# Second feed-forward layer as one block, with fetched and sent expert rows

## The chip, the cores and the metric

The kernel runs on one core of one Trainium2 chip. The metric is the device time of one execution in microseconds (us). Five engines run their own instruction streams and meet only through semaphores: PE (TensorE, matrix products), DVE (VectorE), ACT (ScalarE), POOL (GpSimd, which here also issues every indirect DMA) and SP (SyncE, which only issues DMAs).

## What is computed

Two layers, each a cross-attention and a mixture-of-experts feed-forward, all residual, on 2048 tokens of 256 numbers. The change is in the last part, the feed-forward of the second layer (15 experts, 3 per token, and one shared expert that every token passes):

```
logits = xt @ gate_w.T
scores = jax.nn.softmax(logits, axis=-1)
topk_w, topk_idx = jax.lax.top_k(scores, TOPK)
topk_w = topk_w / (jnp.sum(topk_w, axis=-1, keepdims=True) + 1e-20)
comb = jnp.zeros((T, E), xt.dtype).at[jnp.arange(T)[:, None], topk_idx].add(topk_w)
h = jnp.einsum('td,efd->etf', xt, fc1_w) + fc1_b[:, None, :]
xh, g = (h[..., :F], h[..., F:])
a = jax.nn.gelu(g, approximate=False) * xh * geglu_mult[:, None, :]
yexp = jnp.einsum('etf,edf->etd', a, fc2_w) + fc2_b[:, None, :]
y = jnp.einsum('etd,te->td', yexp, comb)
hs = xt @ s_fc1_w.T + s_fc1_b
xs, gs = (hs[..., :FS], hs[..., FS:])
as_ = jax.nn.gelu(gs, approximate=False) * xs * s_geglu_mult
ys = as_ @ s_fc2_w.T + s_fc2_b
return (y + ys).reshape(s, b, d)
```

with T = 2048, E = 15, TOPK = 3, F = 256, FS = 512.

## The kernel before

Layer 0 (`layer0`, `experts0`) and the attention of layer 1 (`layer1`) come first; they keep the normalised tokens in `XF` (16 tiles of 128 tokens), their transpose in `XFT`, and the residual stream in `X`. Then three blocks follow, each closed by a barrier over all engines.

`route1` ranks the token-expert pairs by expert and gives each a row (slot) in a table of 62 tiles of 128 rows, where every tile belongs to one expert. DVE does the softmax, the top three and the running counts (`pick`, `softmax_top`), PE adds the counts over the partitions (`rk`), DVE turns them into slots. POOL then scatters the rows of `XF` into the table `xs1` in DRAM with 48 indirect DMAs (L1888), 128 rows each. Beside it runs the shared expert: the tokens are cut in four elements `c` of 512 tokens; for each, PE makes four column pieces (`shared_in`, L1905), ACT the gelu, DVE the gated product `AT` (L1986), then PE the second product for four tiles of 128 tokens (`shared_out`, L1917 to L1921, with two short products that add the shared bias and the weighted expert biases), and DVE adds it to `X` (L2034). SP loads the small vectors and shared weights, then the expert weights `W1` and `W2`, all at the start of this block; ACT multiplies `W2` by the gate's factors (L1963).

`experts1` takes the 62 tiles in order. For each, SP loads the rows `XS` (L2079), PE turns them (`turn`, TP, L2101), multiplies by the expert's first weights (`first`, H, L2110), DVE adds the bias (HB, L2191), ACT does the gelu, DVE the product A (L2197), PE turns it (`turn_back`, TA, L2119) and multiplies by the second weights (`second`, Y, L2128), DVE copies Y into `YS` (`keep`, L2204), and POOL stores it into the table `ys1` (L2088). The engines are staggered: in step `s` PE does `turn(s+1)`, `first(s)`, `turn_back(s-1)`, `second(s-2)`, and DVE does `bias(s)`, `gated(s)`, `keep(s-2)`. XS and YS have four buffers each (`DEEP = 4`). The expert of a tile is read into a register by every engine that indexes a weight or a bias with it (`value_load`).

`combine` gathers the three rows of each token from `ys1` with 48 indirect DMAs on POOL (L1234) and DVE adds each times its weight to `X` (L1245); SP stores the result.

The lines that set the order in one step of `experts1`, on SP and on POOL:

```
sp.wait_ge(xt_ready, j - DEEP + 1)
sp.dma_start(XS[:, c, :], xs_tiles[j]).then_inc(xs_loaded[c], 16)

pool.wait_ge(y_done, j + 1)
pool.dma_start(ys_tiles[j], YS[:, c, :]).then_inc(y_stored[c], 16)
```

## Time and profile before

| | us |
|---|---|
| median of 3 runs (1479.38 to 1481.75) | 1479.79 |
| the profiled execution, its own time | 1479.18 |
| span of its records | 1477.4 |
| from the start of routing to the first expert tile | 158.36 |
| the 62 expert tiles | 205.65 |
| from the last expert tile to the end | 73.39 |

A busy time is the sum of an engine's instructions; a wait is an engine's idle time before an instruction, with what ended it. The share of an engine in the whole span says little here, since the layer's three blocks each have a limit of their own: they are read one by one.

### The profile page before, as it was taken

Reading aid. Unit: us, or ns where it says so; the run is one execution under the profiler, and the core shown is the slowest. Engines: PE = TensorE matmul, PEld = TensorE weight load, DVE = VectorE, ACT = ScalarE, POOL = GpSimd, SP = SyncE. Lnnn points to the kernel's source line nnn. Section 1 sums busy time; section 2 is a strip of 40 time slices with the busy share of each in tenths; the row PEclk is TensorE's granted clock in tenths of the full one; section 3 lists DMA queues with packets and bytes.
Section 4 is the critical chain, followed back from the end, with each engine's and each line's share of the span. In section 5 each row is a group of like instructions: output and inputs, shape, how many; then the busy total and the mean of one; then the engine's idle time right before and its main releaser. Section 6 shows DMA issues by size and latency. Waiting matters only on the chain. (4 is left out here: it accounts for less than half of the span.)

```text
span 1477.4 us, 20683 instructions
## 1 busy us (share of the span) xinstructions
PE 1175.2 (80%) x6778; PEld 768.4 (52%) x6779; DVE 732.5 (50%) x1364; ACT 521.5 (35%) x1084; POOL 399.5 (27%) x482
## 2 busy tenths in 40 slices
PE   4798993699999999944698989997539989999900
PEld 2323442699999999932243534443325455555500
DVE  5576622355665556453776676751421124444423
ACT  1285550344543345300265454644130112222200
POOL 3153456223332223023121120000066001111156
PEclk9698655799999999975699999979759999999955
DMA  3460101322333222034232231200853112222134
GB/s 97 171 264 23 51 27 43 109 93 72 112 122 112 82 70 81 19 111 128 72 112 91 73 102 52 66 1 1 261 184 142 54 47 82 82 82 78 64 103 132
DMA packets 86460, 135.49 MB, mean 92 GB/s; under 512 B 18504, under 2 KB 55468, under 8 KB 86258
## 3 DMA queue, kind: packets, MB, share of 16 engines
q1 hardware_dynamic: 72050, 92.58, 19.6%
q0 software_dynamic: 14336, 41.94, 8.2%
q8 instruction: 45, 0.74, 0.2%
q14 instruction: 29, 0.24, 0.1%
HBM read 86.98 MB, written 47.71 MB: 91 GB/s over the span
## 5 line engine op out<-in xcount | busy, mean ns | idle before, releaser
L1744 DVE TENSOR_REDUCE M<-S 128x2 f32<-128x1024 f32 x128 | 153.9, 1221 | 39.2 <-PE S L1389 35.1
L1651 ACT ACTIVATE PT<-S 128x512 f32<-128x512 f32 x256 | 138.8, 594 | 83.1 <-PE S L1413 81.3
L2110 PE MATMUL H<-W,XST 128*128 x248 | 122.1, 616 | 5.2 <-issue 5.1
L222 POOL TENSOR_TENSOR w12l<-stage,w12h 128x1024 fp32r<-128x1024 f32 x28 | 67.9, 2427 | 202.2 <-ACT w12h L216 202.1
L1197 DVE TENSOR_TENSOR HTm0l<-HFm,HTm0h 128x320 fp32r<-128x320 f32 x128 | 121.7, 951 | 1.0
L1203 DVE TENSOR_TENSOR HFm<-Um,SGm 128x320 f32<-128x320 f32 x128 | 62.4, 487 | 80.9 <-ACT SGm L1166 80.6
L1166 ACT ACTIVATE SGm<-Gm 128x320 f32<-128x320 f32 x128 | 55.9, 437 | 119.0 <-PE Um L1124 118.1
L2088 POOL DMA_DIRECT2D ys<-YS x62 | 33.5, 541 | 233.2 <-DVE YS L2204 233.2
L1137 PE MATMUL Ym<-w3h,HTm0h 128*128 128x256 f32 x320 | 93.3, 292 | 0.0
L909 DVE TENSOR_REDUCE M<-S 128x2 f32<-128x1024 f32 x64 | 77.1, 1222 | 30.4 <-PE S L426 29.9
L1389 PE MATMUL S<-KS,QS 48*128 48x512 f32 x256 | 70.3, 547 | 25.7 <-DVE M L1744 9.5
L1137 PE MATMUL Ym<-w3h,HTm0l 128*128 128x256 f32 x320 | 90.4, 283 | 0.0
L1137 PE MATMUL Ym<-w3l,HTm0h 128*128 128x256 f32 x320 | 90.4, 283 | 0.0
L1426 PE MATMUL PV<-PT,VA 128*32 128x256 f32 x1024 | 85.7, 410 | 5.4 <-issue 3.5
L1124 PE MATMUL Gm<-XSTm0h,w12h 128*128 128x320 f32 x256 | 82.2, 321 | 7.9 <-DVE HFm L1203 6.7
L2191 DVE TENSOR_TENSOR HB<-H,B 128x512 f32<-128x512 f32 x62 | 42.9, 692 | 84.5 <-PE H L2110 84.5
L783 ACT ACTIVATE PT<-S 128x512 f32<-128x512 f32 x128 | 69.3, 594 | 32.3 <-PE S L448 31.9
L1124 PE MATMUL Gm<-XSTm0l,w12h 128*128 128x320 f32 x256 | 79.7, 311 | 0.0
L1124 PE MATMUL Gm<-XSTm0h,w12l 128*128 128x320 f32 x256 | 79.7, 311 | 0.0
L1124 PE MATMUL Um<-XSTm0h,w12h 128*128 128x320 f32 x256 | 79.6, 311 | 0.0
L1124 PE MATMUL Um<-XSTm0h,w12l 128*128 128x320 f32 x256 | 79.6, 311 | 0.0
L1124 PE MATMUL Um<-XSTm0l,w12h 128*128 128x320 f32 x256 | 79.6, 311 | 0.0
(273 smaller groups left out, 2485.0 us busy)
## 6 DMA issues: line engine op xcount, KB each, us to landing
stage<-in_W12T SPq DMA_DIRECT2D x32, 512.0 KB, 6.2
xs<-zeros POOLq DMA_DIRECT2D x25, 512.0 KB, 5.9
stage<-in_W3T SPq DMA_DIRECT2D x16, 512.0 KB, 3.8
XS<-xs SPq DMA_DIRECT2D x62, 128.0 KB, 2.0
ys<-YS POOLq DMA_DIRECT2D x62, 128.0 KB, 2.0
W<-in_fc1T SPq DMA_DIRECT2D x2, 3840.0 KB, 21.8
KS<-scrk SPq DMA_DIRECT2D x96, 64.0 KB, 2.3
QS<-scrq SPq DMA_DIRECT2D x96, 64.0 KB, 2.2
```

What stands on the lines that cost most here:

```text
L222: pool.tensor_tensor(ew.part(1, s, c), ew.stage[:, c % STAGES, :], ew.part(0, s, c).bitcast(F32), ALU.subtract).then_inc(ew.low_done, 1)
L783: act.activation(PT[:, at % SLICES, h + j, :], S2[:, j, :], ACT.Exp, scale=(D / H0) ** -0.5).then_inc(exp_done, 1)
L909: dve.tensor_reduce(M[:, n % 3, at:at + TPB + 1:TPB], out[:, :, :], AX.X, ALU.max).then_inc(S1.done(("max", c)), 1)
L1124: m = pe.matmul(bank[:, c % 2, 0:HALF], ew.w12[a][s][:, k, f:f + P], XST[b][:, k, half * HALF:(half + 1) * HALF], start=(k == 0 and (a, b) ...
L1137: m = pe.matmul(Y[:, (s * NTE + i) % 2, 0:D], HT[a][:, j, i * P:(i + 1) * P], ew.w3[b][s][:, j, :], start=(j == 0 and (a, b) == PASSES[0]) ...
L1197: dve.tensor_tensor(HT[1][:, j, at], HF[:, c % HFS, :], HT[0][:, j, at].bitcast(F32), ALU.subtract).then_inc(h_done, 1)
L1203: dve.tensor_tensor(HF[:, c % HFS, :], U[:, c % 2, 0:HALF], SG[:, c % 2, :], ALU.mult).then_inc(hf_done, 1)
L1389: m = pe.matmul(out[:, j, :], QS[at, n % SLOTS1, hp, q * P:(q + 1) * P], KS[at, n % SLOTS1, hp, :], start=True, stop=True)
L1426: m = pe.matmul(PV[VW * h:VW * (h + 1), at], VA[:, b % 2, kt, GH * g + h, :], PT[:, (4 * n + kt) % SLICES, h, at], start=(kt == 0 and part ...
L1651: act.activation(PT[:, at % SLICES, 2 * hp + j, :], S2[:, j, :], ACT.Exp, scale=HP ** -0.5).then_inc(exp_done, 1)
L1744: dve.tensor_reduce(M[:, n % 3, at:at + 2 * TPB + 1:2 * TPB], out[:, :, :], AX.X, ALU.max).then_inc(S1.done(("max", c)), 1)
L2110: m = pe.matmul(H[:, c % 2, :], XST[:, c % 2, k, :], W1[:, k, bass.ds(e, 1), :], start=(k == 0), stop=(k == KD - 1))
```

## The change

`route1`, `experts1` and `combine` become one block, `ffn1`, without a barrier inside.

- The rows of `XF` are stored in token order in DRAM (`xf1`), by SP during the attention (`xf_stored`), and the shared expert's weights and small vectors are loaded there too (`load_shared`); POOL folds the factor into `s2` there. The zero fill of `xs1` in layer 0 (16 DMAs) goes.
- No row is scattered ahead. Instead the routing makes, for each of the 62 tiles, the list of its 128 tokens: DVE marks each pair's partition and tile (`hot`, six chunks), POOL multiplies by the pair's number, PE adds up with one-hot products (`place`, eight products a chunk), and DVE decodes the table into `moves.source` and `moves.target`.
- In the expert loop POOL fetches a tile's rows with an indirect DMA (`fetch`) and sends its results with another (`send`) straight to the row of the pair in `yk1`. The loop's weights and biases are indexed as before; the second bias is added in `keep`, which reads the expert's number too.
- Of the shared expert, elements 0 to 2 are done before the experts (`FRONT = 3`) and element 3 behind them. The two short bias products are gone; the shared bias is added to `X` by POOL (`shared_bias`).
- At the end SP loads the three rows of each token from `yk1` with plain DMAs (16 of 384 KB), and DVE adds them between the pieces of element 3.

```diff
             fills = [(dram, r, min(ZROWS, rows_ - r), done) for dram, rows_, done in (
-                (env.xs0, E0 * CAP0, filled0), (env.xs1, TILES1 * P, filled1)) for r in range(0, rows_, ZROWS)]
+                (env.xs0, E0 * CAP0, filled0),) for r in range(0, rows_, ZROWS)]
 
...
+                for b in range(BATCH):
+                    if t == ends(b) + 6:
+                        sp.wait_ge(xn_done[1], b + 1)
+                        sp.dma_start(env.xf.rearrange("(b t p) d -> b p t d", p=P, t=TPB)[b],
+                                     XF[:, b % 2 * TPB:(b % 2 + 1) * TPB, :]).then_inc(env.xf_stored, 16)
+                if t == 40:
+                    load_shared()
+            sp.wait_ge(env.xf_stored, 16 * BATCH)
...
+FRONT = 3
+HALVES = 2
+CHUNKS = K1 * HALVES
+TC = NT // HALVES
...
-            for t in range(NT):
-                for k in range(K1):
-                    pool.indirect_dma_start(
-                        out=env.xs1[:, :], out_offset=bass.IndirectOffsetOnAxis(ap=env.slot1[:, k, t:t + 1], axis=0),
-                        in_=XF[:, t, :], in_offset=None).then_inc(env.scattered, 16)
...
-                    pe.matmul(pw[:, t % 2, 0:D], env.ones[0:1, :], s2b[:, :], start=False, stop=False)
-
-                    pe.matmul(pw[:, t % 2, 0:D], combT[:, t * P:(t + 1) * P], f2b[:, :],
-                              start=False, stop=True).then_inc(ys_ready, 1)
...
-                if not (isinstance(r, int) and j < DEEP):
-                    sp.wait_ge(xt_ready, j - DEEP + 1)
-                sp.dma_start(XS[:, c, :], xs_tiles[j]).then_inc(xs_loaded[c], 16)
...
+            for k in range(KF):
+                sp.dma_start(W2[:, k, :, :], ins["fc2T"].rearrange("e (k p) d -> k p e d", p=P)[k]).then_inc(w2_loaded, 16)
+            for k in range(KD):
+                sp.dma_start(W1[:, k, :, :], ins["fc1T"].rearrange("e (k p) f -> k p e f", p=P)[k]).then_inc(w1_loaded, 16)
+            sp.wait_ge(decoded, 1)
+            sp.dma_start(B1[:, :, :], ins["fc1_b"].partition_broadcast(P)).then_inc(b1_loaded, 16)
+            sp.wait_ge(expert_done, 1)
+            sp.dma_start(B2[:, :, :], ins["fc2_b"].partition_broadcast(P)).then_inc(b2_loaded, 16)
+
+            sp.wait_ge(h_ready, TILES1)
+            for c in range(DEEP):
+                sp.wait_ge(y_sent[c], LAST_YS[c])
+            for t in range(NT):
+                sp.dma_start(YK[:, t, :, :], env.yk.rearrange("(k t p) d -> t p k d", k=K1, p=P)[t]).then_inc(yk_loaded[t], 16)
+            for i, t in enumerate(finished):
+                sp.wait_ge(fin, i + 1)
+                sp.dma_start(out.rearrange("(t p) d -> t p d", p=P)[t], env.X[:, t, :]).then_inc(sent, 16)
+            sp.wait_ge(sent, 16 * NT)
...
-                pool.dma_start(ys_tiles[j], YS[:, c, :]).then_inc(y_stored[c], 16)
...
+            for i in range(CHUNKS):
+                k, h = divmod(i, HALVES)
+                pool.wait_ge(hot_done, i + 1)
+                wait(pool, hot_free, i - 1)
+                pool.tensor_tensor(HV[:, i % 2, :, :], HI[:, i % 2, :, :],
+                                   env.moves.val[:, k, h * TC:(h + 1) * TC].unsqueeze(2).to_broadcast([P, TC, TILES1]),
+                                   ALU.mult).then_inc(hv_done, 1)
+
+            def fetch(j):
+                if j >= DEEP:
+                    pool.wait_ge(xt_ready, j - DEEP + 1)
+                pool.indirect_dma_start(
+                    out=XS[:, j % DEEP, :], out_offset=None, in_=env.xf[:, :],
+                    in_offset=bass.IndirectOffsetOnAxis(ap=env.moves.source[:, j:j + 1], axis=0),
+                ).then_inc(fetched[j % DEEP], 16)
+
+            def send(j):
                 pool.wait_ge(y_done, j + 1)
-                pool.dma_start(ys_tiles[j], YS[:, c, :]).then_inc(y_stored[c], 16)
-
-            steps(pool, step)
-            for c in range(DEEP):
-                pool.wait_ge(y_stored[c], 16 * ((TILES1 - c + DEEP - 1) // DEEP))
+                pool.indirect_dma_start(
+                    out=env.yk[:, :], out_offset=bass.IndirectOffsetOnAxis(ap=env.moves.target[:, j:j + 1], axis=0),
+                    in_=YS[:, j % DEEP, :], in_offset=None, bounds_check=K1 * TOK - 1, oob_is_err=False,
+                ).then_inc(y_sent[j % DEEP], 16)
+
+            pool.wait_ge(env.xf_stored, 16 * BATCH)
+            pool.wait_ge(decoded, 1)
+            for j in range(DEEP):
+                fetch(j)
+            for c in range(2, BATCH):
+                shared_bias(c)
+            for j in range(TILES1):
+                if j + DEEP < TILES1:
+                    fetch(j + DEEP)
+                send(j)
...
+            def place(i):
+                pe.wait_ge(hv_done, i + 1)
+                for t in range(TC):
+                    m = pe.matmul(table, LO[:, i % 2, t, :], HV[:, i % 2, t, :], start=(i == 0 and t == 0),
+                                  stop=(i == CHUNKS - 1 and t == TC - 1))
+                m.then_inc(hot_free, 1)
+
+            shared_in(0, 0)
+            shared_in(0, 1)
+            pe.wait_ge(run_done, 1)
+            pe.matmul(rk[:, 0:NT, :], env.before[:, :], w.all[:, :, :], start=True, stop=False)
+            pe.matmul(rk[:, 0:NT, :], env.ones[:, :], w.run[:, 0:NT, :], start=False, stop=True)
+            pe.matmul(rk[:, NT, :], env.ones[:, :], w.run[:, NT, :], start=True, stop=True).then_inc(rk_ready, 1)
+            shared_in(0, 2)
+            shared_in(0, 3)
+            place(0)
+            place(1)
+            for q in range(TPB):
+                shared_out(0, q)
+                place(2 + q)
+            for c in range(1, FRONT):
+                for j in range(JS):
+                    shared_in(c, j)
+                for q in range(TPB):
+                    shared_out(c, q)
+
             def turn(r, c):
                 j = r * DEEP + c
-                pe.wait_ge(xs_loaded[c % DEEP], 16 * (r + c // DEEP + 1))
+                pe.wait_ge(fetched[c % DEEP], 16 * (r + c // DEEP + 1))
                 wait(pe, xst_done, j - 1)
                 for k in range(KD):
...
+            pe.wait_ge(at_done, JS * FRONT)
             turn(0, 0)
-            pe.wait_ge(env.w1_loaded, 16 * KD)
+            pe.wait_ge(expert_done, 1)
+            pe.wait_ge(w1_loaded, 16 * KD)
+            pe.wait_ge(shared_done, FIRST)
+            pe.wait_ge(decoded, 1)
...
+            for c in range(FRONT, BATCH):
+                for j in range(JS):
+                    shared_in(c, j)
+                for q in range(TPB):
+                    shared_out(c, q)
...
+            def hot(i):
+                k, h = divmod(i, HALVES)
+                ts = slice(h * TC, (h + 1) * TC)
+                wait(dve, hv_done, i - 1)
+                wait(dve, hot_free, i - 1)
+                dve.tensor_tensor(HI[:, i % 2, :, :], env.iota[:, 0:TILES1].unsqueeze(1).to_broadcast([P, TC, TILES1]),
+                                  sf[:, 1, k, ts].unsqueeze(2).to_broadcast([P, TC, TILES1]), ALU.is_equal)
+                dve.tensor_tensor(LO[:, i % 2, :, :], env.iota[:, :].unsqueeze(1).to_broadcast([P, TC, P]),
+                                  sf[:, 0, k, ts].unsqueeze(2).to_broadcast([P, TC, P]), ALU.is_equal).then_inc(hot_done, 1)
...
+            hot(0)
+            hot(1)
+            shared_gate(0, 2)
+            shared_gate(0, 3)
+            for q in range(TPB):
+                hot(2 + q)
+                shared_add(0, q)
+
+            dve.wait_ge(hot_free, CHUNKS)
+            link(dve.tensor_scalar(far[:, :], table, 0.5, float(FAR), ALU.is_lt, ALU.mult))
+            link(dve.scalar_tensor_tensor(env.moves.target[:, :], table, -1.0, far[:, :], ALU.add, ALU.add))
...
             def keep(r, c):
                 j = r * DEEP + c
+                e = dve.value_load(env.expert[0:1, bass.ds(j, 1)], min_val=0, max_val=E1 - 1)
                 dve.wait_ge(y_ready, j + 1)
                 if not (isinstance(r, int) and j < DEEP):
-                    dve.wait_ge(y_stored[c % DEEP], 16 * (r + c // DEEP))
-                dve.tensor_copy(YS[:, c % DEEP, :], Y[:, c % 2, 0:D]).then_inc(y_done, 1)
+                    dve.wait_ge(y_sent[c % DEEP], 16 * (r + c // DEEP))
+                dve.tensor_tensor(YS[:, c % DEEP, :], Y[:, c % 2, 0:D], B2[:, bass.ds(e, 1), :].squeeze(1), ALU.add).then_inc(y_done, 1)
...
+            for s in final:
+                if s[0] == "in":
+                    shared_gate(s[1], s[2])
+                elif s[0] == "out":
+                    t = s[1] * TPB + s[2]
+                    shared_add(s[1], s[2])
+                    dve.wait_ge(shared_done, t + 1)
+                else:
+                    t = s[1]
+                    dve.wait_ge(yk_loaded[t], 16)
+                    for k in range(K1):
+                        link(dve.scalar_tensor_tensor(env.X[:, t, :], YK[:, t, k, :], env.wt1[:, k, t:t + 1], env.X[:, t, :],
```

POOL in the expert loop before, the body of the hardware loop over four tiles (`ys<-YS` is the store of a tile's results; SP has the loads `XS<-xs`):

```order
L2088 DMA ys<-YS 128x256
L2087 REGISTER_ALU
L2088 ISA
L2088 DMA ys<-YS 128x256
L2087 REGISTER_ALU
L2088 ISA
L2088 DMA ys<-YS 128x256
```

And POOL now, from the end of the routing into the expert tiles (`XS<-xf,source` is `fetch`, `yk<-YS,target` is `send`, `X<-X,s2b` the shared bias):

```order
L1963 DMA XS<-xf,source 128x256 x4
L1948 TENSOR_TENSOR X<-X,s2b 128x1024 x2
L1963 DMA XS<-xf,source 128x256
L1970 DMA yk<-YS,target 6144x256
L1963 DMA XS<-xf,source 128x256
L1970 DMA yk<-YS,target 6144x256
L1963 DMA XS<-xf,source 128x256
L1970 DMA yk<-YS,target 6144x256
```

The loads of the tiles have moved from SP's queue into POOL's, and `fetch(j + 5)` stands behind `send(j)`.

DVE in one expert step before (HB is `bias`, A is `gated`, YS is `keep`):

```order
L2188 TENSOR_LOAD expert
L2188 ISA x2
L2189 REGISTER_ALU
L2191 ISA
L2191 TENSOR_TENSOR HB<-H,B 128x512
L2197 TENSOR_TENSOR A<-HB,GE1e 128x256
L2204 COPY YS<-Y 128x256
```

And now (`hold<-pg,B` is `bias`, `hold<-hold` is `gated`, `YS<-pw,B` is `keep`):

```order
L2251 TENSOR_LOAD expert
L2251 ISA x2
L2252 REGISTER_ALU
L2254 ISA
L2254 TENSOR_TENSOR hold<-pg,B 128x512
L2260 TENSOR_TENSOR hold<-hold 128x256
L2264 TENSOR_LOAD expert
L2264 ISA x2
L2268 ISA
L2268 TENSOR_TENSOR YS<-pw,B 128x256
```

A register load of the expert's number now stands between `gated` and `keep`.

PE at the start of the routing before (`pg<-XFT,s` is `shared_in`, `rk<-B` the counts, `pw<-ident,comb` turns the weights, `pw<-s,AT` and the two behind it are `shared_out`):

```order
L1905 MATMUL pg<-XFT,s 128x512 x16
L1926 MATMUL rk<-B,before 128x240
L1927 MATMUL rk<-B,ones 128x240
L1928 MATMUL rk<-B,ones 128x15
L1935 MATMUL pw<-ident,comb 15x128 x16
L1917 MATMUL pw<-s,AT 128x256 x4
L1919 MATMUL pw<-s2b,ones 128x256
L1921 MATMUL pw<-f2b,combT 128x256
```

And now (`ta<-B,before` and the two behind it are the counts, `ta<-B 128x62` is `place`, `pw<-s,hold` is `shared_out`):

```order
L1994 MATMUL pg<-XFT,s 128x512 x8
L2017 MATMUL ta<-B,before 128x240
L2018 MATMUL ta<-B,ones 128x240
L2019 MATMUL ta<-B,ones 128x15
L1994 MATMUL pg<-XFT,s 128x512 x8
L2010 MATMUL ta<-B 128x62 x16
L2003 MATMUL pw<-s,hold 128x256 x4
L2010 MATMUL ta<-B 128x62 x8
L2003 MATMUL pw<-s,hold 128x256 x4
```

The counts now stand behind half of the first `shared_in`, and the turns of the weights are gone.

## Rows read from the trace of the kernel before

**Rows 1.** Windows: routing with shared expert, expert tiles, combination; columns as its head says.

```profile
core 0: us, PE busy (x) PEld busy (x) DVE busy (x) ACT busy (x) POOL busy (x), PEclk, DMA share, GB/s
1040.00:1198.36 158.36, 112.37 (x342) 62.88 (x343) 39.23 (x130) 26.83 (x52) 50.03 (x52) 0.85 0.44 151
1198.36:1404.01 205.65, 198.50 (x744) 117.44 (x744) 90.22 (x186) 59.27 (x186) 33.00 (x61) 0.98 0.24 77
1404.01:1477.40 73.39, 0.00 (x0) 0.00 (x0) 23.26 (x48) 0.00 (x0) 46.04 (x49) 0.52 0.40 118
```

**Rows 2.** Timeline of the routing: start us, us, what, idle time before.

```profile
1050.48 0.28 DVE L141 TENSOR_TENSOR B<-B 128x120 f32<-128x120 f32 x1
1051.60 15.88 PE L1905 MATMUL pg<-XFT,s 128*128 128x512 f32 x32 [12.17 <-DMA s<-in_s_fc2T]
1068.91 0.16 DVE L1992 COPY B<-rk 128x15 f32<-128x15 f32 x1
1071.25 1.12 DVE L2002 TENSOR_TENSOR B<-iota,B 1x930 f32<-1x930 f32 x1
1076.84 0.19 DVE L2013 CAST slot<-B 128x48 uint32<-128x48 f32 x1
1077.38 1.10 POOL L1888 DMA_INDIRECT xs<-XF,slot  x1 [22.07 <-DVEq L2014]
1083.93 12.07 ACT L1963 ACTIVATE W<-W,mult 128x256 f32<-128x256 f32 x30 [15.72 <-DMA W<-in_fc2T]
1099.06 3.78 PE L1917 MATMUL pw<-s,AT 128*128 128x256 f32 x8 [0.66 <-ACT combT L1966]
```

**Rows 3.** Timeline of PE in one shared element.

```profile
1112.98 14.00 PE L1905 MATMUL pg<-XFT,s 128*128 128x512 f32 x32
1128.54 1.99 PE L1917 MATMUL pw<-s,AT 128*128 128x256 f32 x8 [1.56 <-DVE AT L1986]
1131.52 1.99 PE L1917 MATMUL pw<-s,AT 128*128 128x256 f32 x8
```

**Rows 4.** Timeline of one expert step.

```profile
1387.60 0.38 PE L2101 MATMUL TP<-ident,XS 128*128 128x128 f32 x2
1387.94 1.98 PE L2110 MATMUL H<-W,XST 128*128 x4
1390.07 0.69 DVE L2191 TENSOR_TENSOR HB<-H,B 128x512 f32<-128x512 f32 x1 [1.30 <-PE H L2110]
1391.25 0.43 DVE L2197 TENSOR_TENSOR A<-HB,GE1e 128x256 f32<-128x256 f32 x1 [0.48 <-ACT GE1e L2175]
1391.59 0.42 DVE L2204 COPY YS<-Y 128x256 f32<-128x256 f32 x1
```

**Rows 5.** Line L1234, the gathers of the combination and of layer 1.

```profile
L1234 POOL DMA_INDIRECT YGc<-ys,slot x48: 942/946/1013, 1412.6 to 1471.5; - x48
...
  issue: 17.7, 59
...
DMA to landing us min/median/max: 2.7/2.8/7.3
```

**Rows 6.** Tile expert in the window 1386.5 to 1389.5: register loads, ns, first and last start.

```profile
L2106 PEldq TENSOR_LOAD <-expert x1: 302/302/302, 1387.0 to 1387.0; - x1
L2188 DVEq TENSOR_LOAD <-expert x1: 305/305/305, 1388.2 to 1388.2; - x1
```

**Rows 7.** Windows of 4 us, columns as in the first group.

```profile
668.00:672.00 4.00, 3.09 (x11) 2.20 (x9) 0.80 (x1) 0.00 (x0) 0.00 (x0) 0.79 0.55 170
672.00:676.00 4.00, 0.00 (x0) 0.00 (x0) 3.58 (x9) 0.00 (x0) 0.00 (x0) 0.64 0.00 0
1152.00:1156.00 4.00, 2.47 (x6) 0.76 (x4) 1.29 (x2) 0.69 (x1) 0.00 (x0) 1.00 0.00 0
```

**Rows 8.** DMA issues: count, KB each, median us from issue to landing.

```profile
ctxT<-in_ctxT SPq DMA_DIRECT2D x8, 512.0 KB, 4.5
```

**Rows 9.** Timeline, the last addition of the combination.

```profile
1474.31 0.48 DVE L1245 SCALAR_TENSOR_TENSOR X<-YGc,wt,X 128x256 f32<-128x256 f32 x1 [0.72 <-DMA YGc<-ys,slot]
```

**Rows 10.** The page's groups of instructions, one of POOL.

```profile
L222 POOL TENSOR_TENSOR w12l<-stage,w12h 128x1024 fp32r<-128x1024 f32 x28 | 67.9, 2427 | 202.2 <-ACT w12h L216 202.1
```

More of the change, by code:

```diff
@@ L1619, in _ @@
                         root(b, 1)
+                if t == 90:
+                    pool.wait_ge(env.shared_loaded, 16 * 6)
+                    for j in range(FFS // P):
+                        ins_ = pool.tensor_scalar(env.s2[:, j, :], env.s2[:, j, :], smul[:, j:j + 1], None, ALU.mult)
+                    link(ins_)
         @block.scalar
@@ L2058, in experts1 @@
         LOOPS = (TILES1 - HEAD) // DEEP
+        LAST_YS = {c: 16 * ((TILES1 - c + DEEP - 1) // DEEP) for c in range(DEEP)}
         def steps(eng, step):
@@ L2068, in steps @@
                 step(j // DEEP, j % DEEP)
-        xs_tiles = env.xs1[:, :].rearrange("(j p) d -> j p d", p=P)
-        ys_tiles = env.ys1[:, :].rearrange("(j p) d -> j p d", p=P)
+        back = [("in", c, j) if p == 0 else ("out", c, j) for c in range(FRONT, BATCH) for p, j in
+                [(0, j) for j in range(JS)] + [(1, q) for q in range(TPB)]]
+        each = -(-NT // len(back))
+        final, todo = [], list(range(NT))
+        for i, s in enumerate(back):
+            final.append(s)
+            if i >= 1:
+                final += [("rows", t) for t in todo[0:each]]
+                todo = todo[each:]
@@ L2073, in _ @@
+        final += [("rows", t) for t in todo]
+        finished = []
+        for i, s in enumerate(final):
+            for t in range(NT):
+                mine = [("rows", t)] + ([("out", *divmod(t, TPB))] if t >= FIRST else [])
+                if s in mine and all(m in final[0:i + 1] for m in mine):
+                    finished.append(t)
         @block.sync
         def _(sp):
-            def step(r, c):
-                j = r * DEEP + c
-                if not (isinstance(r, int) and j < DEEP):
-                    sp.wait_ge(xt_ready, j - DEEP + 1)
-                sp.dma_start(XS[:, c, :], xs_tiles[j]).then_inc(xs_loaded[c], 16)
@@ L2094, in _, with shared_in @@
+            for c in range(2, BATCH):
+                shared_bias(c)
+            for j in range(TILES1):
+                if j + DEEP < TILES1:
+                    fetch(j + DEEP)
+                send(j)
         @block.tensor
         def _(pe):
+            def shared_in(c, j):
+                i = c * JS + j
+                wait(pe, at_done, i - 1)
+                for half in range(2):
+                    for k in range(KD):
+                        m = pe.matmul(pg[:, 2 * (i % 2) + half, :], s1[:, k, half * FFS + j * P:half * FFS + (j + 1) * P],
+                                      XFT[:, k, c * SEQ:(c + 1) * SEQ], start=(k == 0), stop=(k == KD - 1))
+                m.then_inc(gs_ready, 1)
@@ L2180, in _ @@
             turn_back(*divmod(TILES1 - 1, DEEP))
+            act.wait_ge(a_done, TILES1)
+            for c in range(FRONT, BATCH):
+                for j in range(JS):
+                    gelu(c, j)
         @block.vector
         def _(dve):
-            dve.wait_ge(env.b1_loaded, 16)
+            link = Link(dve, chain)
+            pick(dve, link, env, w, E1, K1, env.lg[:, :, :], False)
+            dve.nop().then_inc(lg_sub, 1)
+            dve.wait_ge(ex_done, 1)
+            softmax_top(dve, link, env, w, E1, K1, 0.0)
```

408 lines of the change are left out of this document (176 added, 232 removed).

## Prediction

> **What bounds it now.** I read the windows of the three parts first. In the routing [rows 1] PE is busy 112 of 158.4 us, at a mean clock of 0.85; in the expert tiles it is busy 198.5 of 205.65 us at 0.98, so the tiles are PE's, 205.65 / 62 = 3.3 us each with the ends; in the combination PE does nothing for 73.4 us. Then the timeline of the routing says where PE's missing time is [rows 2]: it starts at 1051.6, 12.2 us late, because the shared weights were asked for only in this block; it has nothing from the end of the ranks (1068.9) until 1099.06, since the second shared product stands behind the weights' turns and those behind ACT, which waited for `W2` until 1083.93 and then scaled for 12.07 us. The combination is 48 gathers on POOL, each 0.946 + 0.30 us (17.7 us in 59 idles) = 1.25 us [rows 5]: 60 us, plus barrier, first landing and last store.
>
> **Routing and elements 0 to 2: 158.4 becomes 87.9 us.** The shared weights now load in the attention, whose length I leave alone: one more megabyte and a half beside its loads, and four short POOL products where POOL waits. So PE starts at 1040.3 instead of 1051.6. The softmax and counts of DVE are as before, done at 1050.48 + 0.28 = 1050.8 [rows 2]. Counts on PE and two gates of some 0.7 (512 columns, as HB [rows 4]) give 1052.4 for the first slot operation. Before, slots took 1068.91 to 1077.03 = 8.1 us; the two operations of 1.12 over the 930 pairs and two short ones go behind (-2.7), three small casts come in (+0.8): 1058.6. Then the marks. One chunk is DVE 496 + 1024 columns, at the 1.12 per 930 of that row 0.6 + 1.2 = 1.8 us; POOL 2.43 x 496 / 1024 = 1.2 us [rows 10]; PE 16 short records, more than nothing and less than two `shared_out` pieces of 8 records (4.0 [rows 3]), for which I take 1.7, as they have 62 columns and not 256. Two chunks and two gates: 1063.6. The other four go in rounds with a `shared_out` piece: two chunks are in flight, and a round is a piece (2.0), its addition (0.4) and what of DVE, POOL and PE is not hidden by them, near 4.0 us: 1079.6, and 1.2 for the last one: 1080.8. Elements 1 and 2 cost 14.0 + 1.56 + 4 x 2.0 = 23.6 us each (a piece was 1131.52 - 1128.54 = 2.98 with its bias products, now 1.99) [rows 3]: first turn at 1128. Hidden under them: the decoding on DVE (about 5 us), the scaling on ACT, weights (all landed 44 us after the block's start before), both bias loads. Without that cover ACT's 12.07 us would show. Gain 1198.4 - 1127.9 = 70.5, between 64 and 77 by the rounds (2.5 to 5.5 us each).
>
> **The expert tiles: 205.65 becomes 310 us.** PE, ACT and DVE do the same work; what changes is who loads. Before, SP fetched four tiles ahead and waited only for `turn`. Now POOL must first send: `fetch(j+5)` is queued behind `send(j)`, which waits for `keep(j)`, done in step j+2, and the rows are wanted by `turn(j+5)` at the start of step j+4. So two steps must hold one whole round trip. From the start of a step:
>
> - turn to H: 0.34 in the row [rows 4]. There PE had read the expert's number at 1387.0 [rows 6], ahead of the turn; H came 0.94 after the read. Behind a turn that had to wait, the sequencer cannot have read ahead, so I take 0.95.
> - H to the start of HB: 2.13. HB to the end of A: 1.61. A's end to YS's end: 0.33 [rows 4].
> - `keep` now reads the register first. The read of the next step started 0.2 after A did [rows 6] and takes 0.31, with register work behind it: +0.4, between 0 (if it hides under A) and 0.75 (as long as on PE).
> - DVE to POOL: slots ended at 1077.03, POOL's DMA began 1077.38: 0.35.
> - the send, first after a wait, 1.10 + 0.30 = 1.40 [rows 2, 5].
> - the fetch from its start to its landing: 2.8 [rows 5]; to PE 0.1.
>
> Sum 10.07 us for two steps, 5.03 a tile, against 3.25 before. POOL itself is busy only 2.65 us of it. The first four tiles are ahead: three steps of 3.3, then the fifth at 9.9 + 10.07 = 20, tile 61 at 20 + 28 x 10.07 = 302, and 7.3 us to the last YS as before, plus 1.0 for the two reads: 310.3. Loss 104.6. The ends of the sum are 8.8 (0.34 to H, no price for `keep`'s read, 1.25 for the send, 2.7 for the landing), a loop of 272, and 10.9 (0.75, and 0.5 more in landing and waits), a loop of 333.
>
> Of the fetch's 2.8 us the row is a gather of the same 128 rows of 1 KB. The Trainium skill (DMA: Bandwidth & Descriptors, "Anatomy of one DMA") gives a POOL-issued DMA about 2.0 us and its bytes at 436 GB/s, an estimate of 2.3 us here. By it the two steps would be 9.6 and the loop 14 us shorter; the measured row decides.
>
> **The clock.** PE has 3.2 us of work in a tile of 5.03 and so stops for 1.8. A stop of 1.53 in 4 us left the clock at full (1152 to 1156) [rows 7]. A stop that began before 672 brought it down within 672 to 676, mean 0.64 [rows 7]. Stops here are between, and at first they come in pairs as 3.3 and 6.8 us steps, with the whole slack in one. A tile at the lower of the two levels (1.2 of 2.4 GHz) has 6.4 us of PE work, 1.4 more than the round trip allows it. None to 57 tiles: 0 to 78 us. The step near the border makes some fall likely, and full work at the low clock brings it back, so I take ten tiles, 14 us.
>
> **Element 3 and the combination: 73.4 becomes 39.7 us.** From the last YS: the last send's start 0.35 and landing 2.8, then 384 KB by SP, less than the 4.5 of 512 KB [rows 8], 3.6: first rows at 6.8. PE meanwhile makes two pieces of element 3 (14.0 / 4 each), with gelu and gate 8.6; the rows stand behind the second gate in DVE's order. Then DVE is the bound: 48 additions of 0.48 + 0.04 = 25.0, two gates 1.5, four additions 1.8: 36.9. From the last addition to the end 1477.4 - 1474.79 = 2.6 [rows 1, 9], plus 0.2. Gain 33.7. It hides PE's 22 us of element 3; if the clock is low when it starts, 3 us come out.
>
> **The sum.** Profiled execution 1479.18 (span 1477.4, 1.8 around it; the median of the runs is 0.6 above): - 70.5 + 104.6 - 33.7 + 14 = +14.4: 1493.6, 1494 in terms of the runs. The zero fills that go away (16 DMAs in layer 0) cost POOL 0.5 each where it waits; I give them nothing.
>
> **Rivals.**
>
> - *The round trip is shorter and the change wins.* The place is `send` before `fetch` on POOL, the price 28.5 us per microsecond of the two-step sum. With 8.8 and no fall of the clock: 1479.2 - 70.5 + 66.7 - 33.7 = 1442. It decides below 9.9 us when the clock stays up. For it speaks that the stops of 1.5 us did no harm; against it that the reads' time is seen in the row.
> - *Nothing is late.* If rows were there whenever PE turns to them, the tiles cost 3.3 us and the time is 1479.2 - 104.2 = 1375. Only the program's order speaks against it, but strongly: 3.3 x 2 = 6.6 us cannot hold 1.4 + 2.8 and the 5.4 of the step's chain.
> - *The clock stays low through the tiles*: 310 + 78: 1558. Against it: at the low clock a step of 6.4 us has almost no stop, and steps without a stop ran at 0.98 before [rows 1].
> - *DVE holds POOL's issues up.* Each tile has two indirect DMAs beside three DVE operations; if each waits out one of 0.42 to 0.69 us, the two steps grow by 1.1: 1494 + 31 = 1525. The gathers of the combination ran beside DVE additions at 942 to 1013 ns [rows 5], so the trace does not show it.
>
> The last rival is a rule of the Trainium skill (SBUF — State Buffer, the box on the "DVE blocks DMA" trap): a DVE operation in its two-port mode locks POOL out of writing descriptors. By that rule the loop is slower still; the trace has no such case.
>
> **Chances.** My forecast (two-step sum of 9.4 to 10.9 with a part of the tiles at low clock) 0.62, alone 1470 to 1530. Shorter round trip 0.20, nothing late 0.05, clock low 0.09, DVE holding POOL 0.04. Leaving out 1375 and the lower tail of the shorter trip below, and the low clock above, the range is 1448 to 1538. A measurement of this kernel tells a difference of about 0.2% from none. Faster by more (below 1476.8): both faster rivals and 0.03 of the forecast, 0.28. Same: 0.06 of it. Slower: 0.66.
>
> **What would show it.** Right: in the tiles TP waits for the DMA `XS<-xf` for over 1 us a tile, the tile costs 4.7 to 5.6 us, POOL's send begins 0.3 to 0.4 after YS, and PE's clock is below 0.98; first TP near 1128; DVE gapless at the end. Wrong: TP waits for nothing (nothing late), TP to H stays 0.3 (the read's price is not there), or the first TP comes after 1140, which would be a stall in the marks that I did not see.

## The result and the profile after

The kernel after takes 1563.97 us (median of 4 runs, 1560.82 to 1568.82), the kernel before 1480.77 us in 4 runs beside it: a ratio of 1.056, interval 1.0521 to 1.0599. The forecast was 1494 us, its range 1448 to 1538.

The three parts of the kernel after by windows, cut at the first turn of the tiles and at the end of the last YS (columns as in [rows 1]):

```profile
1040.00:1135.60 95.60, 85.05 (x305) 54.82 (x305) 48.32 (x135) 21.90 (x44) 19.73 (x14) 0.89 0.53 191
1135.60:1523.80 388.20, 271.72 (x745) 143.95 (x743) 96.12 (x187) 63.94 (x186) 118.40 (x119) 0.78 0.12 36
1523.80:1564.60 40.80, 21.62 (x64) 11.83 (x64) 27.70 (x56) 2.75 (x4) 1.54 (x2) 0.86 0.64 206
```

Against [rows 1] the routing ends 62.8 us sooner and the combination is 32.6 us shorter, but the tiles take 388.2 us in place of 205.65. They are 6.26 us each, and the mean granted clock of 0.78 says that PE was at the lower of its two levels (1.2 of 2.4 GHz) for a good part of them. The waits of that window show who waits for whom (line, what it waited for, us in total, times, longest):

```profile
DVE hold L2254 <- PE pg L2047: 230.5, 62, 9.3
POOL yk L1970 <- DVE YS L2268: 229.0, 52, 10.3
...
PE pg L2038 <- DMA XS<-xf,source: 99.4, 29, 6.3
```

The last row is `turn` waiting for its rows: 99.4 us in 29 waits. The timeline shows that from the sixth tile on every second turn waits, 3.4 us in the mean (2.6 to 4.3, and one of 6.3). The second row is the queue's other side: POOL stands at `send` for 229 us with the next fetch behind it. One pair of tiles in the timeline shows the whole circle (start, duration, engine, line, operation, idle time before it and what ended it):

```profile
1253.58 0.69 PE L2038 MATMUL pg<-ident,XS 128*128 128x128 f32 x2 [3.47 <-DMA XS<-xf,source]
...
1254.67 3.77 PE L2047 MATMUL pg<-W,hold 128*128 x4 [0.41 <-ACT hold L2129]
...
1258.68 0.69 DVE L2254 TENSOR_TENSOR hold<-pg,B 128x512 f32<-128x512 f32 x1 [7.08 <-PE pg L2047]
...
1259.90 0.38 PE L2038 MATMUL pg<-ident,XS 128*128 128x128 f32 x2
1259.93 0.43 DVE L2260 TENSOR_TENSOR hold<-hold 128x256 f32<-128x256 f32 x1 [0.56 <-ACT hold L2148]
1260.12 1.88 PE L2047 MATMUL pg<-W,hold 128*128 x4
...
1260.88 0.42 DVE L2268 TENSOR_TENSOR YS<-pw,B 128x256 f32<-128x256 f32 x1 [0.53 <-issue]
...
1262.11 1.01 POOL L1970 DMA_INDIRECT yk<-YS,target  x1 [7.40 <-DVE YS L2268]
...
1263.43 1.16 POOL L1963 DMA_INDIRECT XS<-xf,source  x1 [0.30 <-issue]
...
1266.51 0.69 PE L2038 MATMUL pg<-ident,XS 128*128 128x128 f32 x2 [3.42 <-DMA XS<-xf,source]
```

Read it as a ring: turn (L2038), H (L2047), bias (L2254), A (L2260), YS (L2268), send (L1970), fetch (L1963), turn: 12.93 us for two tiles, a *trip*. The first tile comes out of a stop of 3.47 us, and its H takes 3.77 us: the low level. The next tile, 5.5 us later, has its H in 1.88 us: the full one. Then PE stops again. It is so to the end of the loop: H takes 3.4 to 3.8 us behind 28 of the 29 stops (the other is recorded in two parts) and 1.88 us in the tile that follows. So the clock comes back within a tile of work, as I had assumed, but only to fall with the next stop.

In front, one thing was not in the forecast. The start of the routing in the timeline:

```profile
1042.78 4.69 POOL L1948 TENSOR_TENSOR X<-X,s2b 128x1024 f32<-128x1024 f32 x2 [8.75 <-POOLq L1268]
1042.79 2.47 DVE L108 COPY B<-logits 128x240 f32<-128x240 f32 x1 [0.32 <-PEq L1268]
...
1045.30 0.40 DVE L109 TENSOR_REDUCE B<-B 128x16 f32<-128x240 f32 x1
...
1045.74 2.00 DVE L110 TENSOR_TENSOR B<-B 128x240 f32<-128x240 f32 x1
```

In the trace of before the copy L108 took 0.28 us and the subtraction L110 0.41, and POOL did nothing then. Here POOL adds the shared bias to two elements in 2 x 2.35 us, and each of the two DVE operations ends 0.13 and 0.27 us behind one of these, while the reduction between them is as short as ever.

### The profile page after: what moved, and what is told of

Read it like the earlier page. It is cut to its first block and busy times, and to the rows that moved or that the text cites. A ratio compares the mean times of both kernels' runs of the same rounds, so it can differ in the third digit from the quotient of the medians.

```text
span 1564.6 us, 20604 instructions
## 1 busy us (share of the span) xinstructions
PE 1240.5 (79%) x6794; PEld 794.7 (51%) x6795; DVE 753.8 (48%) x1377; ACT 524.2 (34%) x1080; POOL 405.8 (26%) x443
## 5 line engine op out<-in xcount | busy, mean ns | idle before, releaser
L2047 PE MATMUL pg<-W,hold 128*128 x248 | 169.8, 822 | 14.7 <-ACT hold L2129 10.2
L1675 ACT ACTIVATE PT<-S 128x512 f32<-128x512 f32 x256 | 138.8, 594 | 89.2 <-PE S L1414 87.3
L2254 DVE TENSOR_TENSOR hold<-pg,B 128x512 f32<-128x512 f32 x62 | 42.9, 692 | 230.5 <-PE pg L2047 230.5
L1970 POOL DMA_INDIRECT yk<-YS,target x62 | 62.8, 1013 | 252.1 <-DVE YS L2268 229.0
L2038 PE MATMUL pg<-ident,XS 128*128 128x128 f32 x124 | 30.6, 336 | 99.8 <-DMA XS<-xf,source 99.4
L2148 ACT ACTIVATE hold<-hold 128x256 f32<-128x256 f32 x62 | 25.8, 416 | 208.1 <-DVE hold L2254 208.1
L2047 PEld LDWEIGHTS pg<-W,hold 128*128 128x128 f32 x248 | 56.4, 252 | 71.1 <-issue 71.0
L1414 PE MATMUL S<-QS,KS 64*128 64x512 f32 x256 | 76.1, 462 | 5.1 <-DMA QS<-NM 4.8
```

Source lines behind the costliest of these rows:

```text
L1414: pe.matmul(S2[:, j, :], KS[at, n % SLOTS1, hp, kt * P:(kt + 1) * P], QS[at, n % SLOTS1, hp, :], start=True, stop=True).then_inc(s2_ready, 1)
L1675: act.activation(PT[:, at % SLICES, 2 * hp + j, :], S2[:, j, :], ACT.Exp, scale=HP ** -0.5).then_inc(exp_done, 1)
L1970: pool.indirect_dma_start(out=env.yk[:, :], out_offset=bass.IndirectOffsetOnAxis(ap=env.moves.target[:, j:j + 1], axis=0), in_=YS[:, j % D ...
L2047: m = pe.matmul(H[:, c % 2, :], XST[:, c % 2, k, :], W1[:, k, bass.ds(e, 1), :], start=(k == 0), stop=(k == KD - 1))
```

## The experiments

Each time stands beside runs of the kernel before on the same chip. The first four experiments ran on one chip (before: 1480.66 us), e5 to e8, e9 to e12 and e13 to e15 on three more, on which before takes 1542.0 to 1544.4 us. So times are compared on one chip, and loops of different chips by their traces. "Loop" is the stretch from the first turn to the end of the last YS, 388.2 us in the kernel after. How it hangs on the trip: the forecast's sum is loop = 18.2 + 29 x trip, where 18.2 is the steps ahead of the first trip (9.9) and the end (7.3 + 1.0). By it 388.2 us is a trip of 12.76 us for two tiles; from the first waiting turn (1152.23) to the last (1510.64) it is 12.80.

### Sends three tiles behind (e1), and again on another chip (e9)

```
for j in range(TILES1 + 3):
    if j + DEEP < TILES1:
        fetch(j + DEEP)
    if j >= 3:
        send(j - 3)
```

> Edit: on POOL the send of tile j - 3 stands behind the fetch of tile j + 4, in place of the send of tile j; nothing else differs from the kernel after. Theory (the loop is bound by the round trip through the send that stands ahead of the fetch): a fetch now waits for nothing that ends later than the turn of four tiles before it, so TP never waits for the DMA, the clock is near 0.98 and the tiles cost 3.3 us each, as in the kernel before: the loop goes from 388 to about 206 us, the time to about 1382 us. Rival 1 (the transfers themselves are too slow or DVE holds up POOL's descriptors, wherever they stand in the queue): TP still waits and the loop stays over 280 us, the time above 1455. Rival 2 (POOL's 2.65 us a tile beside 0.3 us waits becomes the bound): 3.5 to 4 us a tile, 1395 to 1425.

> The lag-3 kernel once more, as the measure for the kernels beside it on the same chip: the kernel before came to 1481 us on the chip of the first four runs and to 1542 us on that of the next four. On the first chip it was 1383.15 us; the loop should be 205.6 us of it on any chip.

Measured: 1383.15 us, ratio 0.935 (0.9326 to 0.9374); on the other chip 1409.84 us, ratio 0.914 (0.9108 to 0.9172). The loop is 205.6 us in both traces. Its window and the group of H (busy us, mean ns of one, idle before) on the first chip:

```profile
1134.60:1340.20 205.60, 199.10 (x745) 116.69 (x743) 96.00 (x187) 59.27 (x186) 119.53 (x119) 1.00 0.23 68
```

```profile
L2048 PE MATMUL pg<-W,hold 128*128 x248 | 120.9, 610 | 4.1 <-issue 1.1 <-ACT hold L2130 0.6 <-DVE hold L2255 0.3
```

No turn waits for the DMA any more, and a record of H takes 610 ns in the mean where the kernel after has 822. The same two indirect DMAs of the same size are issued on the same engine in the same number, so neither their speed, nor POOL's 1.9 us of busy time a tile, nor DVE's operations beside them made the loss. It was which instruction stood ahead of the fetch. The register read in `keep` is still there too, and costs nothing now.

### Sends one tile behind (e2)

The same edit with 1 in place of 3.

> Edit: as the kernel after, but the send of tile j - 1 stands behind the fetch of tile j + 4. Theory: three steps in place of two hold one round trip. The trip read in the trace after is 12.6 us with H at the low clock and about 10.7 at the full one: 3.6 us a tile at the full clock (loop 222 us, time 1398), 4.2 us at the low one (loop 261, time 1437). Stops would be about 1 us in three tiles, so I expect the clock above 0.9 and a time of 1390 to 1415. Rival (the transfers are slow by themselves): no better than the kernel after, 1560.

Measured: 1405.97 us, ratio 0.9482 (0.9461 to 0.9502); loop 228.6 us at a clock of 1.00, 3.69 us a tile. Three steps hold a trip of 3 x 3.69 = 11.1 us, against 10.9 worked out below for the full clock. PE is idle for 24.7 us of the loop, in pieces of at most 1.0 us (5 of them turns that wait for rows), and the clock does not fall in them. This is the place where the forecast's rule "so many steps hold one trip" is seen at a second size.

### Work for PE in its stops (e3, e13)

```
for _ in range(3):      # four in e13
    pe.matmul(TP[:, c % 2, D:2 * D], env.ident[:, :], XFT[:, 0, 0:D], start=True, stop=True)
pe.wait_ge(fetched[c % DEEP], 16 * (r + c // DEEP + 1))
```

> Edit: the kernel after with three more products of 128 x 256 ahead of each turn's wait for its rows, into a part of PSUM that nobody reads (some 1.5 us of PE work a tile, no part of the result). Theory (it is the low clock of the tile after each stop that made 388 us of the forecast 310): PE hardly stops any more, H takes 1.9 us instead of 3.8 in every tile, the two steps hold 10.7 us, and the loop falls to about 332 us although work was added, the time to about 1508 us, clock above 0.93. Rival (the round trip is longer for another reason, and the clock is a mere sign of it): the waits shrink but the loop stays at 375 to 390 us, the time at 1550 to 1567; if PE's work is on the path, it grows by up to 93 us.

> Edit: as the run with fillers, with four products of 128 x 256 ahead of each turn's wait in place of three (some 1.95 us of PE work a tile). It tells the share of the clock from that of the trip: with three the loop was 352 us at a clock of 0.95. Theory (at the full clock the two steps hold the 10.07 us of the forecast and the 0.5 us of the bounds check, some 10.8): clock 0.98 or more and a loop of 18.2 + 29 x 10.8 = 331 us, up to 340, so the low clock alone makes 50 to 57 of the 388 us. Rival (the clock was never more than part: PE's own 5.2 us a tile now bounds the pair, or the trip is 11.5 us at any clock): 350 us or more.

Measured: e3 1521.85 us, ratio 1.0261 (1.0237 to 1.0285), loop 352.2 us at a clock of 0.95, between the 332 of its theory and the 375 of its rival: with three fillers 26 turns still wait, up to 4.0 us. e13 1544.71 us, ratio 1.0009 (0.9993 to 1.0025), loop 340.7 us at 0.99. The kernel after (e15, the same chip as e13):

> The kernel after, on the same chip as the run with four fillers. Its loop should be 380 to 395 us at a clock of 0.78 to 0.80 here as well; the ratio to before is 1.056 on a chip like the first, and nearer 1.03 on one where before takes 1542 us.

It took 1590.87 us, ratio 1.0318 (1.0281 to 1.0355), with a loop of 388.2 us at 0.78. So 1.9 us of useless PE work in each tile made the kernel 46 us faster. The windows of the two loops, e13 and then e15:

```profile
1160.30:1501.00 340.70, 310.73 (x1233) 207.28 (x1231) 95.59 (x186) 65.08 (x186) 117.82 (x119) 0.99 0.14 41
```

```profile
1159.90:1548.10 388.20, 269.59 (x745) 142.92 (x743) 96.03 (x187) 63.73 (x186) 118.49 (x119) 0.78 0.12 36
```

PE is busy 41 us more and the loop is 47.5 us shorter. That shows the low clock as a cause and not only as a companion of the stops. The 47.5 us are a lower bound of its share, since e13 is nearly PE's own loop (310.7 of 340.7 us busy); 340.7 is just past the 340 that I had given as the top.

### Without the second bias's register read (e4)

```
-                e = dve.value_load(env.expert[0:1, bass.ds(j, 1)], min_val=0, max_val=E1 - 1)
...
-                dve.tensor_tensor(YS[...], Y[...], B2[:, bass.ds(e, 1), :].squeeze(1), ALU.add)
+                dve.tensor_tensor(YS[...], Y[...], B2[:, 0, :], ALU.add)
```

> Edit: as the run with fillers, and keep adds the second bias of expert 0 for every tile, so that DVE reads no register ahead of YS (the result has the wrong second bias). Theory: keep's register read is on the path and costs 0.4 us in a round trip of two tiles, so 31 x 0.4 = 12 us less than the run with fillers; between 0 (the read hides while DVE waits for Y) and 31 x 0.75 = 23 us less.

This kernel has the fillers of e3; it leaves the read out and adds expert 0's bias to every tile. Measured: 1505.57 us, ratio 1.0171 (1.015 to 1.0191), 16.3 us less than e3 on the same chip; 12 was expected. Over 29 trips that is 0.56 us each. The loops of the two traces differ by more, 28 us, because the traced execution of e3 was its slowest (1529.23 us, clock 0.95 in the loop) and that of e4 its fastest (1500.11, 0.99). The operations themselves settle the price. A and YS in one tile of e4:

```profile
1303.21 0.42 DVE L2262 TENSOR_TENSOR hold<-hold 128x256 f32<-128x256 f32 x1 [0.48 <-ACT hold L2150]
1303.56 0.42 DVE L2269 TENSOR_TENSOR YS<-pw,B 128x256 f32<-128x256 f32 x1
```

From A's end to YS's end it is 0.35 us here, as in the kernel before (0.33), and 0.36 in the mean of e4's trips, against 0.90 in e3's and 0.91 in those of the kernel after. The read is on the path and costs 0.54 us a trip; 0.4 was forecast.

### Without the scatter's bounds check (e8, e12)

```
-                    in_=YS[:, j % DEEP, :], in_offset=None, bounds_check=K1 * TOK - 1, oob_is_err=False,
+                    in_=YS[:, j % DEEP, :], in_offset=None,
```

with `yk` longer by spare rows, one for each unused slot, so that these slots are now written.

> Edit: the run with fillers on PE (1521.85 us), and the scatter has no bounds check: the unused slots are written to spare rows behind yk. It tests why a send starts 0.81 us after YS ends and not the 0.35 of my sum. Theory (the check's own register work stands between the wait and the descriptors): 0.35 us, 31 x 0.46 = 14 us less: 1508. Rival (0.81 us is what the way from DVE to a DMA of POOL costs here, with or without the check): within 4 us of 1522, or a little longer, since unused rows are written too.

> Edit: the kernel after, in its own order, and scatters without the bounds check: one term of the two-step sum alone, without the fillers. The trip of a pair of tiles falls by 0.52 us. Theory (the trip sets the loop, at whatever clock): 31 x 0.52 = 16 us less than the loop of 388, or some 25 us if the shorter stops also let the clock up in a part of the tiles. Rival (the clock is what holds the pair at 12.5 us, with PE's work in it): under 8 us.

In the kernel after a send that waits for YS begins its DMA 0.78 to 0.82 us after YS ends, 0.81 in nearly all. Without the check it is 0.27 to 0.29 us in both runs, but for the very last send (0.35). One trip of e8 at the full clock:

```profile
1302.35 0.43 PE L2040 MATMUL pg<-ident,XS 128*128 128x128 f32 x2 [0.40 <-DMA XS<-xf,source]
...
1303.47 1.98 PE L2049 MATMUL pg<-W,hold 128*128 x4 [0.69 <-ACT hold L2131]
...
1305.68 0.69 DVE L2260 TENSOR_TENSOR hold<-pg,B 128x512 f32<-128x512 f32 x1 [3.54 <-PE pg L2049]
...
1306.93 0.43 DVE L2266 TENSOR_TENSOR hold<-hold 128x256 f32<-128x256 f32 x1 [0.56 <-ACT hold L2150]
...
1307.89 0.42 DVE L2274 TENSOR_TENSOR YS<-pw,B 128x256 f32<-128x256 f32 x1 [0.53 <-issue]
...
1308.59 0.99 POOL L1970 DMA_INDIRECT yk<-YS,target  x1 [3.91 <-DVE YS L2274]
...
1309.88 0.97 POOL L1963 DMA_INDIRECT XS<-xf,source  x1 [0.30 <-issue]
...
1312.73 0.44 PE L2040 MATMUL pg<-ident,XS 128*128 128x128 f32 x2 [0.59 <-DMA XS<-xf,source]
```

E8 took 1522.5 us, ratio 0.9887 (0.9844 to 0.993), on a chip other than e3's, so the two times are not to be compared; its loop is 318.5 us at 0.99, a trip of 10.36 us. E12, in the order of the kernel after, took 1566.51 us, ratio 1.013 (1.0099 to 1.0162), loop 364.5 us at 0.79: 23.7 us less than 388.2, for 29 x 0.52 = 15 us of shorter sends. The turns' waits fell from 99.4 to 77.6 us in as many waits. No part of the gain is the clock's: H to the bias takes 3.91 us in the mean of e12's trips and 3.89 in those of the kernel after. What is left lies in YS to send, where two late sends near the end of the loop were late by less, and in fetch to turn (2.85 against 3.02 in the mean). So one shorter term alone does not free the loop of the low clock.

### The front: late shared bias, spread loads, two elements (e5, e6, e7)

All three start from the kernel with sends three behind. E5:

```
-            for c in range(2):
-                shared_bias(c)
+            pool.wait_ge(run_done, 1)
+            shared_bias(0)
```

and `shared_bias(1)` goes behind the first fetches, to the elements 2 and 3.

> Edit: the lag-3 kernel (1383.15 us), and POOL adds the shared bias to element 0 only when DVE's counts are done, to element 1 after the marks. Theory (the copy of the logits took 2.47 us in the trace after and 0.28 before, the subtraction 2.00 and 0.41, because POOL's two additions of 4.69 us hold DVE up): both are back at 0.28 and 0.41, the counts come 3.8 us sooner, the first TP near 1131, the time 3 to 4 us shorter: 1379.5 us. Rival 1: the addition now holds up the slot operations or the marks by as much, no change. Rival 2: the two long DVE operations have another cause (the shared product on PE, the weights' loads) and stay.

Measured: 1403.27 us, ratio 0.9099 (0.9072 to 0.9127) against 0.914 (0.9108 to 0.9172) for the plain kernel on another such chip: the intervals overlap. The trace settles it: L108 takes 0.29 us and L110 0.41, and from the copy of the logits to the first turn it is 90.5 us against 93.4 in e9 and 93.5 in e1: 2.8 to 2.9 us less, not 3.8. A part came back: the addition, now at 1075.13, holds up `L2198`, which takes 0.85 us and took 0.17. The Trainium skill (SBUF — State Buffer, "Who interferes with whom") has DVE and GpSimd share one pair of ports, which the one that issues first holds for a whole instruction. These durations agree with it: the 2.47 and 2.00 us are the rest of a POOL operation (2.34 and 1.73 us) and 0.13 and 0.27 us more. It is the direction opposite to the one I had priced.

E6: the six loads of shared weights at steps 44, 50, ... 74 in place of all at step 40.

> Edit: the lag-3 kernel, and SP issues the six loads of shared weights one at a time at steps 44, 50 ... 74 of the attention in place of all six at step 40. Theory (SP needs 8.1 us for the six issues, so the copy NM to QS queued behind them comes late and PE stops 4.3 to 4.8 us at 797 to 802, with a low clock after it): no stop for QS, the attention ends 2.5 to 3 us sooner, 1380.5 us. Rival (the bytes, or the stores of xf, are what lengthens the attention): within 1 us of 1383.15.

Measured: 1410.83 us, ratio 0.9151 (0.913 to 0.9171): no gain. The stop of PE for `QS` is gone, but the attention ended at 1071.84 where e5, e7 and e8 on the same chip ended theirs at 1063.69 to 1067.23. From one copy of logits to the next (948.67 to 1020.53) e6 takes 71.9 us, where e5, e7 and e8 take 66.6. The stretch from 1000 to 1045, first in e6 and then in e5:

```profile
1000.00:1045.00 45.00, 41.81 (x264) 19.76 (x262) 16.70 (x27) 24.04 (x46) 2.07 (x6) 0.77 0.04 13
```

```profile
1000.00:1045.00 45.00, 40.71 (x314) 18.30 (x310) 17.72 (x31) 28.18 (x53) 2.09 (x6) 0.92 0.04 13
```

PE was busy in both, and did 264 records at 0.77 and 314 at 0.92. So the stop was taken away, and its time and more was lost at a lower clock later on; why the clock is lower there, in the same part of the attention, stays open.

E7: `FRONT = 2`.

> Edit: the lag-3 kernel with two shared elements in front of the experts and two behind. In front 22.6 us go. Behind, DVE's 36 us are no longer what is longest: PE has 2 x 22 us, the two elements' last gate and addition, so the tail goes from 41 to about 54 us: 1383 - 22.6 + 13 = 1374 us. Rival 1: the scaling of W2 on ACT and the weights' loads, which the front hid, now show: 1383 or more. Rival 2: W1 is not there by the first turn, +10 us.

Measured: 1396.62 us, ratio 0.9051 (0.9033 to 0.9069), the shortest of e5 to e8. From the logits to the first turn it is 70.9 us, 22.5 less than in e9; from the last YS to the end 52.5 us, 11.3 more than in e1 (13 was expected). A second element behind costs half of what it saves in front, because PE's work then fills time in which DVE alone was busy.

### Both together, and without the check (e10, e11)

> Edit: lag-3 kernel with two shared elements in front and the late shared bias. Theory (both gains are in different places: 22.7 us less in front and 11.3 more behind in the run with two elements, 3.0 us less by the late bias): 14.5 us below the lag-3 kernel on this chip. Rival (the counts that come sooner meet a PE that is still in the first product, and the weights' landing becomes what the first turn waits for): only 10 to 12 us.

> Edit: as the run with two elements and the late bias, and scatters without the bounds check. With sends three tiles behind, the loop is PE's at 3.3 us a tile, so the 0.52 us that each send gains should be worth nothing: within 1 us of that run. Rival (POOL at about 3.0 of 3.3 us a tile holds PE up now and then): up to 4 us faster.

Measured: both 1392.3 us, ratios 0.9018 (0.8993 to 0.9043) and 0.9012 (0.899 to 0.9035). That is 17.5 us below the lag-3 kernel beside them (14.5 expected; the traces of e10 and e9 have 25.3 us less in front and 11.2 more behind, 14.1 in all, and the rest is spread ahead of the routing). The bounds check is worth nothing once the send is off the path: a cost is a cost only where something waits for it. This version beats before by 10% on this chip.

### The kernel before on another chip (e14)

> The kernel before, for its trace on this chip, since its time was 1481 us on one chip and 1542 us on two others while the loop of the lag-3 kernel was the same 205.6 us on all. If this chip is one of the slow ones, the expert tiles should be 205 us here too and the 60 us lie elsewhere; which part they lie in I don't know.

Measured: 1544.14 us in one run, beside a median of 1544.43. From the first turn to the end it is 278.0 us, against 279.0 on the first chip; the rest lies ahead, see the last section.

## Why the forecast was wrong

Direction, bound and mechanism were right; the size was not. Against the profiled execution (1566.38 us; 1493.6 forecast) the 72.8 us fall so:

| part | forecast | measured | difference |
|---|---|---|---|
| up to the first turn (first turn at) | 1127.9 | 1135.6 | 7.7 |
| tiles, clock included | 310.3 + 14 | 388.2 | 63.9 |
| from the last YS to the end | 39.7 | 40.8 | 1.1 |

**The step that failed is the clock's term**: "I take ten tiles, 14 us". E8 ran its trips at 0.99 and 10.36 us; with the 0.52 us of the bounds check that is 10.88, a loop of 18.2 + 29 x 10.88 = 333.7 us. So the low clock makes at most 388.2 - 333.7 = 54.5 us of the loop, and at least the 47.5 that e13 gave back: 33.5 to 40.5 us more than the forecast's 14. The trips say the same from inside: H to the bias takes 4.01 us in the pair shown and 2.21 in e8's. In the mean of all trips it is 3.89 and 2.23, and 29 x 1.66 = 48 us. The 6 us between 48 and 54.5 are in fetch to turn and in late sends, not in PE.

The argument in the forecast was that full work brings the clock back. It does, within a tile. What I missed is that the falls repeat. I had written that the steps "at first" come in pairs of 3.3 and 6.8 us with the whole slack in one, and then counted as if the slack evened out, with stops of 1.8 us in place of 3.6. It does not: the two sends of a pair stand 3.35 us apart on POOL (1262.11 and 1265.46), the two fetches behind them too, and the next pair of tiles starts as the last did. So PE stops for 3.4 us in every second tile to the end, and every such stop costs a tile at the low level: 29 tiles, not ten.

The rival *the clock stays low through the tiles* gave 310 + 78 = 388 us for the loop. That number was met by coincidence: by its mechanism every tile is at the low level with almost no stop, and the trace shows every second one, with stops. Its 78 us stand for 48 to 54.5 of the clock and 23 of a longer trip.

**The two-step sum** was 10.07 us and is about 10.9 at the full clock, at the upper of its bounds (8.8 to 10.9). Term by term, from the trip of e8: turn to H 1.12 (0.95 forecast), H to HB 2.21 (2.13), HB to A's end 1.68 (1.61), A's end to YS's end 0.95 (0.33 + 0.4), send to fetch 1.29 (1.40), fetch to turn 2.85 (2.8 + 0.1). The one term off by much is from YS to the send, 0.81 in the kernel after against 0.35: I took it from a DMA without a bounds check [rows 2]. The sum is 10.88 - 10.07 = 0.81 us longer (the two 0.81 are equal by chance), 29 x 0.81 = 23 us in all, 13 of them by that term. The register read on DVE was there and on the path, with 0.54 us for the forecast's 0.4. Two slips in the forecast's own sums changed nothing: a trip of 10.9 gives a loop of 334 us and not 333, and a microsecond of the sum costs 29 us and not 28.5.

**The front.** The first slot operation came 7.3 us late (1059.69); the marks took 2.7 us more than worked out (the last ended at 1090.8), the two elements 2.3 less. The 7.3 us are the attention's end, 2.8 us later in this trace (1042.25 against 1039.46 for the copy of the logits), and the 3.8 us by which POOL's additions held DVE; 0.7 us are left over. The first is partly chance: e1 to e4, with the same attention, ended it at 1038.6 to 1041.3. One stop in it is real: PE waits 4.3 to 4.8 us for `QS`, behind the six issues of the shared weights, and in e6, where these are spread, it does not. The forecast named "four short POOL products where POOL waits", and not the two long additions at the start of the block.

**The combination** came as forecast: DVE almost without gaps, 48 additions in 23.3 us, 40.8 us in all.

**The rivals.** *Shorter round trip* fell with a trip of 10.9 us at the full clock. *Nothing late* needs another order on POOL, and is then what happens: e1. *DVE holds POOL's issues up* is refuted: sends of 1013 ns and fetches of 985 in the kernel after, 1013 and 1004 in e1, where nothing is lost. Nor does any run show that an operation of the loop takes both ports, on which the rule named beside this rival rests.

## What to carry to other kernels

When a queue is handed over to an engine that must first do something else, count how many steps hold the new round trip, and put the waiting instruction as far behind the issuing one as the buffers allow: here the order of two instructions on POOL turned +5.6% into -6.5%. When a trip comes out longer than the steps that hold it, look at where the slack collects, not at its mean: in e2 stops of at most 1.0 us cost only themselves, here stops of 3.4 us in every second tile cost another 1.7 us each. An elementwise operation that is put on POOL "for free" is to be checked against what DVE does at that moment.

## What the runs showed that I had not expected

**Useless work paid.** Fillers of 1.9 us a tile took 46 us off (e13 against e15).

**The bounds check of an indirect DMA** costs 0.52 us between the end of the awaited YS and the DMA (0.81 against 0.29 us), and hardly anything shows it in the DMA's own record (1013 against 989 ns).

**The same kernel differs by 4% between chips, and not evenly.** Before takes 1481 us on one chip and 1542 to 1544 on three; the kernel with sends three behind takes 1383 and 1410. The loops are alike to 0.1 us. In e14 the attention ends 25.7 us later (logits at 1065.20). A part of that is in the first layer, where PE is as busy at a lower clock; 150 to 200 us in e14 and then in before on the first chip:

```profile
150.00:200.00 50.00, 46.19 (x253) 20.07 (x256) 24.22 (x65) 21.33 (x40) 17.17 (x27) 0.50 0.11 39
```

```profile
150.00:200.00 50.00, 46.08 (x300) 19.47 (x297) 25.34 (x73) 27.52 (x51) 23.04 (x31) 0.65 0.11 40
```

The other 39.5 us lie in the routing of before, between the scatters' start and the first turn. There additions of the first shared element come late, while POOL issues its 48 scatters (1102.8 to 1163.5). The first two start 16.8 and 23.4 us after both their product and DVE were ready, some 40 us together (`remote` is an end of a wait that no engine or DMA of this core explains):

```profile
1146.64 0.42 DVE L2034 TENSOR_TENSOR X<-pw,X 128x256 f32<-128x256 f32 x1 [40.51 <-remote]
1170.46 0.76 DVE L2034 TENSOR_TENSOR X<-pw,X 128x256 f32<-128x256 f32 x2 [23.39 <-remote]
```

On the first chip these additions followed PE at once, beside the same scatters. No run here tells the cause. The kernel after has no such scatters, and e15 differs from the first trace of it only ahead of the routing (24.3 us). That is why the change costs 5.6% on one chip and 3.2% on another.
